# Eight loads of the second stream's weights and context issued from ScalarE's queue instead of SyncE's, in a six-block decoder on one Trainium2 core

## What is computed

```python
x = _layernorm(x + _L0_attn_ref(x, ...))                       # Mamba: scan over time, 512 x 16 states
x = _layernorm(x + _L0_xattn_ref(x, ctx_1024, itok, ...))      # sparse latent attention, 64 chosen keys a query
x = _layernorm(x + _L0_ffn_ref(x, ...))                        # two quantised linears, GELU between
x = _layernorm(x + _L1_attn_ref(x, ...))                       # self attention, 16 heads of 16
x = _layernorm(x + _L1_xattn_ref(x, ctx_1024, Wq, Wkv, Wo, bo)) # cross attention, 16 heads of 64
x = _layernorm(x + _L1_ffn_ref(x, router_w, ...))              # mixture of 8 experts (top 6) and a shared one
```

## Time and profile before

| | |
|---|---|
| median of 3 runs | 3802.04 us (3790.84 to 3803.64) |
| the profiled execution | 3786.92 us, span of its trace 3785.1 us |
| PE busy | 3170.1 us, 84% |
| DVE busy | 2833.4 us, 75% |
| ACT busy | 2083.7 us, 55% |
| POOL busy | 922.6 us, 24% |
| moved by DMA | 338.71 MB, 89 GB/s, 26% of the DMA engines' time |

### The profile page before, as it was taken

How to read it: one execution, slowest core, us unless ns; L and a number is a source line. 1 busy time by engine, 2 the same in 40 slices (tenths; PEclk the granted TensorE clock), 3 DMA queues, 4 the chain that set the end, 5 groups by cost and what they waited for, 6 DMA issues and landing times.

```text
span 3785.1 us, 59632 instructions
## 1 busy us (share of the span) xinstructions
PE 3170.1 (84%) x22658; PEld 2253.3 (60%) x22658; DVE 2833.4 (75%) x4915; ACT 2083.7 (55%) x4816; POOL 922.6 (24%) x740
## 2 busy tenths in 40 slices
PE   2568988898898989889898998889889888988877
PEld 1345656666565666656566665666656566665655
DVE  4687786868778687877868778786877868687622
ACT  3356656565665656566464655656566565556432
POOL 1423050221404122140411305031230503114000
PEclk8689999999999999999998999999999999999988
DMA  5212141422304142130413214041331404133110
GB/s 190 81 62 94 32 142 45 147 71 80 129 21 154 52 138 80 56 129 33 166 52 130 88 43 141 34 161 57 116 102 32 153 34 155 62 104 107 48 42 17
DMA packets 208286, 338.71 MB, mean 89 GB/s; under 512 B 24480, under 2 KB 177568, under 8 KB 193280
## 3 DMA queue, kind: packets, MB, share of 16 engines
q1 hardware_dynamic: 208000, 334.90, 25.9%
HBM read 311.75 MB, written 20.97 MB: 88 GB/s over the span
## 4 chain that ended last, share of the span: by engine, by line
PE 49%; DVE 28%; ACT 15%; issue 6%; POOL 0%; SPq 0%; DMA 0%; DVEq 0%; ACTq 0%
PE ps L636 5%; PE ps L888 5%; DVE nm L1567 4%; PE ps L617 4%; PE ps L949 4%; PE ps L803 3%; PE ps L789 3%; PE ps L779 3%; ACT ps L1070 2%; PE ps L834 2%; PE ps L648 2%; DVE region_x L1544 2%; ACT region_y L1219 2%; PE ps L556 2%; DVE region_x L1524 2%
## 5 line engine op out<-in xcount | busy, mean ns | idle before, releaser
L1331 POOL TENSOR_TENSOR region_x<-region_x 128x512 f32<-128x512 f32 x512 | 646.4, 1274 | 357.7 <-DVE region_x L1544 356.5
L1544 DVE TENSOR_TENSOR_SCAN region_x<-ps,region_x 128x512 f32<-128x512 f32 x512 | 614.9, 1214 | 72.7 <-ACT ps L1070 72.3
L1070 ACT ACTIVATE ps<-region_x,aneg 128x255 f32<-128x255 f32 x1024 | 440.0, 474 | 332.7 <-DVE region_x L1544 329.5
L1311 POOL TENSOR_TENSOR region_x<-region_x 128x512 f32<-128x512 f32 x96 | 121.7, 1268 | 1184.0 <-ACT region_x L1018 1179.0
L1323 POOL TENSOR_TENSOR region_x<-region_x 128x512 f32<-128x512 f32 x128 | 162.7, 1271 | 1003.7 <-DVE region_x L1524 861.7
L1567 DVE TENSOR_REDUCE nm<-ps 128x4 f32<-128x1024 f32 x256 | 305.6, 1220 | 62.6 <-PE ps L617 58.8
L888 PE MATMUL ps<-xTy,wide 128*128 128x256 f32 x1280 | 316.5, 397 | 1.4 <-DVE region_y L1731 1.4
L1219 ACT ACTIVATE region_y<-ps,rmax 128x256 f32<-128x256 f32 x512 | 235.8, 496 | 119.1 <-DVE rmax L1672 119.1
L888 PEld LDWEIGHTS ps<-xTy,wide 128*128 128x128 f32 x1280 | 244.2, 197 | 36.1 <-DVE region_y L1731 1.6
L1672 DVE TENSOR_REDUCE rmax<-ps 128x4 f32<-128x1024 f32 x128 | 152.3, 1221 | 147.4 <-PE ps L815 147.4
L1524 DVE TENSOR_TENSOR region_x<-region_x,ps 128x512 f32<-128x512 f32 x384 | 255.7, 666 | 3.8 <-PE ps L556 3.3
(11 more groups left out here) (251 smaller groups left out, 6924.9 us busy)
## 6 DMA issues: line engine op xcount, KB each, us to landing
region_x<-rows_of_dt SPq DMA_DIRECT2D x1024, 128.0 KB, 2.8
wide<-in_wgate SPq DMA_DIRECT2D x16, 1280.0 KB, 8.2
wide<-in_wup SPq DMA_DIRECT2D x16, 1280.0 KB, 10.9
down<-in_wmoe SPq DMA_DIRECT2D x16, 1280.0 KB, 7.0
wide<-in_wq SPq DMA_DIRECT2D x16, 1024.0 KB, 5.4
wide<-in_wk SPq DMA_DIRECT2D x16, 1024.0 KB, 7.5
wide<-in_wv SPq DMA_DIRECT2D x16, 1024.0 KB, 9.6
down<-in_wo SPq DMA_DIRECT2D x16, 1024.0 KB, 12.6
```

The costliest lines, as they stand in the source:

```text
L1070: last = f(ps[:, 1 + 2 * (k % 2), half * T + 1:(half + 1) * T], dt_rep[k % SLOTS][:, 1:T], ACT.Exp, scale=aneg[:, k, half:half + 1])
L1331: nc.gpsimd.tensor_tensor(hbuf[k % HSLOTS], hbuf[k % HSLOTS], csb, ALU.mult).then_inc(hc_ready, 1)
L1544: nc.vector.tensor_tensor_scan(flat(hbuf[k % HSLOTS]), ps[:, 1 + 2 * (k % 2), :], flat(hbuf[k % HSLOTS]), 0.0, ALU.mult, ALU.add).then_inc ...
```

## The change

The functions `load_ctx`, `load_wide_cross` and `load_wide_moe` take the issuing engine as an argument. The eight loads of a round leave SP for ACT, each behind a wait of its own or behind an ACT instruction whose wait covers it:

- `ctxT` of sequence i+2 behind the fourth V eviction (L1199), ahead of the copy of `xTy` (L1001);
- `wgate`, `wup` behind the fourth Q eviction (L1205), ahead of the first exponentials (L1219);
- `wmoe` ahead of the norm behind cross attention, with a wait for the output projection (`Y.sum_ps`), which stands ahead of that norm's table load;
- `wq2`, `wk2`, `wv2` and `wo2` ahead of the norm behind the experts, with waits for the last up projection (`up_ps`) and for the down projection (`Y.sum_ps`).

SP keeps X's transfers and the store. At the start of the program all first loads stay on SP.

```diff
 ORDER = {
-    "sp": (123, "x19 y2 x2 y1 x25 y2 x2 y1 x23"),
+    "sp": (123, "x48 y1 x23"),
...
+        def load_ctx(eng, i):
+            eng.dma_start(ctxT[:, i % 2], dram["ctxT"][i].rearrange("a p d -> p a d")).then_inc(ctx_loaded[i % 2], 16)
+
+        def load_wide_cross(eng):
+            for dst, name in ((wq2, "wq2"), (wk2, "wk2"), (wv2, "wv2")):
+                eng.dma_start(dst, dram[name]).then_inc(wide_cross, 16)
+
+        def load_wide_moe(eng):
+            for dst, name in ((wgate, "wgate"), (wup, "wup")):
+                eng.dma_start(dst, dram[name]).then_inc(wide_moe, 16)
...
             def second_half(i):
                 yield
-                if i + 2 < B:
-                    sp.wait_ge(att2.proj, at(i, 12, 8))
-                    load_ctx(i + 2)
-                yield
-                sp.wait_ge(att2.proj, at(i, 12, 12))
-                load_wide_moe()
-                yield
-                sp.wait_ge(Y.sum_ps, at(i, 3, 2))
-                sp.dma_start(wmoe, dram["wmoe"]).then_inc(down_moe, 16)
-                yield
-                if i + 1 < B:
-                    sp.wait_ge(up_ps, at(i, 5, 5))
-                    load_wide_cross()
-                yield
-                if i + 1 < B:
-                    sp.wait_ge(Y.sum_ps, at(i, 3, 3))
-                    sp.dma_start(wo2, dram["wo2"]).then_inc(down_cross, 16)
-                yield
                 sp.wait_ge(batch_done, i + 1)
...
                     f(VV[:, n // 2, n % 2 * 512:(n % 2 + 1) * 512], ps[:, b, :], ACT.Copy).then_inc(a.vevac, 1)
+                if i + 2 < B:
+                    load_ctx(act, i + 2)
                 yield
                 xT_copy(Y, xTy, 7, at(i, 3, 2))
...
                     f(QT2[:, 2 * n:2 * n + 2, :], bank(b), ACT.Copy, scale=0.125).then_inc(a.evac, 1)
+                load_wide_moe(act)
...
                 yield
+                act.wait_ge(Y.sum_ps, at(i, 3, 2))
+                act.dma_start(wmoe, dram["wmoe"]).then_inc(down_moe, 16)
                 rstd_guess_of(Y, i, c, 2)
...
                 yield
+                if i + 1 < B:
+                    act.wait_ge(up_ps, at(i, 5, 5))
+                    load_wide_cross(act)
+                yield
+                if i + 1 < B:
+                    act.wait_ge(Y.sum_ps, at(i, 3, 3))
+                    act.dma_start(wo2, dram["wo2"]).then_inc(down_cross, 16)
                 rstd_guess_of(Y, i, c, 3)
```

More of the change, by code:

```diff
@@ L341, in load_choices @@
                 sp.dma_start(idx[:], dram["idx"][i]).then_inc(idx_loaded, 16)
[L343 to L352, removed]
             def first_half(i):
@@ L437, in _ @@
             sp.dma_start(hmv1, dram["hmv1"]).then_inc(staged, 16)
-            load_ctx(0)
+            load_ctx(sp, 0)
             for name, shape, _ in RESIDENT[FIRST:]:
                 sp.dma_start(W[name][:], dram[name]).then_inc(w_rest, 16)
-            load_ctx(1)
-            load_wide_cross()
+            load_ctx(sp, 1)
+            load_wide_cross(sp)
             sp.dma_start(wo2, dram["wo2"]).then_inc(down_cross, 16)
```

## The result

The changed kernel is slower: median 3812.8 us of 13 runs (3802.5 to 3820.6) against 3797.7 us of 13 runs of the kernel before (3785.5 to 3805.2), ratio 1.0041 with a 95% interval of 1.0029 to 1.0053. That is 15 us, some 1 us for each of the fourteen rounds in which the cross weights are loaded anew while Mamba runs. The profiled execution of the changed kernel has a span of 3811.0 us.

The account below looks back on a forecast made before the run. It took the chain of PE, DVE and ACT to bound the kernel, with SP and transfers off it. Terms 6.6 + 0 + 0 + 0 = 6.6 us on a 3802.0 us median gave 3809 us, range 3788 to 3828.

Parts of the forecast that it names:

- what I called likeliest: Whole kernel: a measured time within 0.3% of 3809 us, counted as the same; chance 0.58.
- What bounds the kernel: PE, busy 84%, with DVE and ACT holding 92% of the chain; SP and transfers off it, so freeing them gains nothing.
- The term for ctxT: Between fourth V eviction and xTy copy, ACT's issue delays PE 0.47 us in 14 rounds: 6.6 us, bounds 0 to 14.7.
- wgate and wup: Behind the last Q eviction, two ACT issues lie under 4.10 us of idle time: 0 us.
- the cross loads' issues: Before the norm behind the experts, three issues lie in 9.00 us of ACT idle and wo2's also fits: 0 us.
- wmoe and the table load behind its wait: Before the norm behind cross attention, issue plus table load, 1.73 us, fit into 1.79 us: 0, at most 5 us.
- Rival 1: On ACT, at ctxT and wmoe, issues are dearer or wait for the datapath: 20 us slower, 3822 us; chance 0.22.
- Rival 2: Earlier cross weights delay X's spread feeding POOL ahead of L761: 4.3 us a round, 64 us slower, 3866 us; chance 0.04.
- The sign that I gave for this rival: In the profile after the change, ACT or DVE would be seen waiting for a spread; no size given.
- Rival 3: Freed SP and POOL move DVE or PE by 1 us in each of 14 rounds: faster, 3788 us; chance 0.13.
- rival 4: At the norm behind cross attention, the table load behind the new wait is uncovered: 26 us slower, 3828 us; chance 0.03.
- The spread by PE's clock: Rounds differ by up to 2 us with PE's clock; 0.8 us over fifteen rounds is 12 us, either way.

Follow-up runs that it names:

- the late loads: Changed kernel with ACT issuing the four cross-attention weight loads later, behind Mamba's decay of unit 9; ratio 1.0004 to the kernel before.
- `k == 1`: Changed kernel with wo2 still issued by ACT, but placed behind Mamba's decay of unit 1; ratio 1.0052 to the kernel before.

## Why the prediction was right or wrong

The range held, 3788 to 3828 with 3812.8 measured, and the point, 3809, was 4 us off. But what I called likeliest was a difference within 0.3%, and the kernel is slower by 0.41%; and the 6.6 us that I added came from a place that costs nothing. The number was near for a wrong reason.

*What bounds the kernel.* Right: SP and transfers were off the chain, and freeing them brought nothing, as the late loads show with SP and POOL both free. (ACT's wait of 2.2 us, which I counted to the steady rounds, lies in the first sequence, and I named three kinds of waits and not four; nothing hangs on it.)

*The term for ctxT, 14 x 0.47 = 6.6 us.* Wrong: it is 0, the lower bound. An issue on ACT took 0.39 us and ran beside the eviction. The rule that I weighed and did not follow, of the Trainium skill ("PSUM — Partial Sum Buffer", Engine vs sequencer instructions), had it right: ACT's sequencer executes the issue while the datapath evicts (issue at 2138.18, eviction from 2138.17 to 2138.77), and in the run with wo2 behind four decays it even went ahead of them. The nearest row I had was one of SP, which computes nothing, and so could not show an issue beside computing work.

*wgate and wup; the cross loads' issues.* Right as far as ACT goes, 0.

*wmoe and the table load behind its wait.* Right, 0. The cover was larger than I worked out: the issue took 0.33 us and not 0.45 and began 0.18 us ahead of DVE's addition, and 0.32 us were left over. The drain of 1380 ns that the Trainium skill puts behind a switch ("ScalarE: Activation LUTs", What ACT_TABLE_LOAD costs) did not appear: 1.28 + 0.32 us lie between the start of the load and y_lnv, and the 0.32 were a wait for DVE.

*Rival 1, dearer issues on ACT, 0.22.* Wrong: they took 0.33 to 0.46 in the median and 3.1 us together a round, where the eight medians on SP make 3.9; five were cheaper than on SP and three (wup, wk, wv) dearer by 0.02 to 0.03.

*Rival 2, the spreads beside the weights, 0.04.* This is what happened, mechanism and place: unit 7's spread, POOL, the sum, L761's slack. Its sizes were off. The landing was 8.0 to 10.5 us and not 12.5. It was also allowed more than 6.4 us: in the round of the rows the spread was issued at 1822.43 and not at 1823.8, which gives 7.7, of which the slower issues beside the weights take back 0.4. So POOL was 1.8 us late and not 6.1. And the sum itself took up to 0.87 us longer at the lower clock, which I had not thought of; without that, the mean delay of 1.8 us would just have fitted in the 1.85 us of slack, and only the four rounds with 2.2 to 3.3 us would have lost by it. Together 1 us a round in place of 4.3, in fourteen rounds and not fifteen. The step that failed is the sentence against it: that three loads with a lead of 5 us and a queue of their own do little harm. I had worked out the point from which it decides, a landing of 8.2 us, and had in the same rows a landing of 12.5 behind the same 4 MB; a threshold that lies below the worst case seen deserved far more than 0.04. I also gave all thought to the 3 MB, which alone are harmless (1.0000), and none to wo2, which was to be issued 2 us ahead of that spread. The Trainium skill's sentence that transfers of several issuers interleave on the same 16 engines ("DMA: Bandwidth & Descriptors", Issuing engines are not separate DMA queues) agrees with what the runs show: the first spread of the run landed in 10.4 us and not 7.4 when wo2 was issued 2.3 us behind it in the other queue. I had read from it that the overlap would be cheap. The sign that I gave for this rival, ACT or DVE waiting for a spread, was the wrong one: in the changed kernel they do so in one round, for 0.6 and 0.7 us, and it was POOL that waited.

*Rival 3* fell with the late loads (1.0004), *rival 4* with the row of y_lnv. *The spread by PE's clock* was right in kind and too small: I had rounds differ by up to 2 us, and in one execution they took 222.2 to 227.0, six in a row 225.3 or more.

## What to carry to other kernels

Moving transfers to another engine's queue frees the first queue, but it also lets them start earlier, and the transfers that stay now share the DMA engines with them. Before such a move, list what will be in flight during each burst of small transfers that others wait for, in bytes, and look for the first one that an in-order engine waits on; here 4 MB were too much beside a spread with 8 us to spare, and 3 MB were not. If it is too late, move the consumer: one product moved down in POOL's order did as much (0.9991) as any other order of the loads (0.9994 to 1.0004).

## What was not expected of the hardware

- An issue of a transfer on ACT takes 0.33 to 0.46 us for 256 KB to 1.3 MB and cost the instructions around it nothing that shows (the copy behind it started 0.49 us behind the eviction, 0.50 without it): it ran beside the one ahead of it, and in the run with `k == 1` 0.34 us ahead of decays that stand before it in the program.
- A transfer of 128 KB that lands in 2.8 us alone landed 8.0 to 10.5 us behind its issue with 4 MB in the other queue, the last of them issued 2.3 to 3.4 us ahead of it. With the last one issued 2.3 us behind it, such a transfer took 10.4 us in the median.
- PE's granted clock was 0.50 over sixteen matmuls behind 5.3 us of idle and 1.00 behind 1.96 us; behind 3.6 us both occurred (1.94 and 1.07 us for the sixteen), in other rounds of the same executions, and so they did behind 2.8 us in the run with POOL's order changed.
